# A two-layer graph network on one core: destination rows loaded a quad at a time, index loads spread over three quads, and the last layer's bias on TensorE

## The chip, the core and the metric

The kernel runs on one core of one Trainium2 chip. The core has TensorE (matmuls, PE in the profile), VectorE (DVE), ScalarE (ACT), GpSimd (POOL) and SyncE (SP), which here only issues transfers. The metric is device time in microseconds (us), less is better.

## The reference

There are 6250 nodes with 128 features, 200000 edges sorted by destination, and 128 features for each edge. Two layers follow each other, each with a residual and a layer norm of its own.

```python
src, dst = edge_index
# layer 0
m_in = concat([h_node[src], h_node[dst], h_edge])
m    = silu(m_in @ msg_W1 + msg_b1) @ msg_W2 + msg_b2
agg  = segment_sum(m, dst)
h0   = layernorm(x + (silu(concat([x, agg]) @ upd_W1 + upd_b1) @ upd_W2 + upd_b2)) * gamma + beta
x1   = layernorm(x + h0)
# layer 1
agg  = segment_sum(x1[src], dst) / max(degree, 1)
h    = relu(relu(concat([x1, agg]) @ W1 + b1) @ W2 + b2)
out  = layernorm(x1 + h)
```

## The kernel before

**Stages.** First (up to about 76 us) the products P = x·W(source part) and Q = x·W(destination part) of all nodes are made and stored in HBM as `P_d` and `Q_d`. Then one pass goes over the edges. An edge tile is 128 edges, a quad is 4 tiles (`QT`), a group is 7 quads (`GQ`), there are 391 quads (`NQ`) in 56 groups (`GROUPS`). The loop variable `s` is the quad, `g, q = divmod(s, GQ)`. Nodes are in blocks of 128.

**One quad.** TensorE makes `ps_pre` (`products`, L1135 for the edge features, L1138 for the destination part by `Qw`, a window of rows of Q, times the 0/1 matrix `nodeE`). VectorE adds the gathered rows of P (L948, `pre<-ps_pre,gath`), ScalarE takes the silu (L1328), and TensorE sums the hidden rows by destination (`sums`, L1172, L1174). TensorE also counts, for layer 1, how many edges run from each node to each window of destinations (`count`, L1152), ScalarE copies the counts (L1288), and SyncE stores them as `A_d` (L766). VectorE makes the 0/1 matrices `edgeL` and `edgeK` (L933, L935) and `nodeE` (L925) from keys that `make_keys(g + 1)` (L900 to L909) builds once a group at q == 2 from `src_i`, `dst_i` and `first_i`.

**Loads.** GpSimd gathers rows of P for group g + 1, four for each quad (L876, an indirect DMA each): for quad q once the vector add of quad q of group g is done (it frees `gath[:, q]`), the first also once `src_i` is there. All other loads of the pass are issued by SyncE in the order of its program and lie in one queue: `rel_c` and `eT_c` for chunks of two quads (L759, L761, the latter waits for `pre_mm`, TensorE's products), at q == 1 `load_ids(g + 1)`: `src_i`, `dst_i`, `first_i` (L749 to L751) and then `load_q(g + 1)`, which reads a start row from the table `gbase` into a register (L740) and loads `Qw` in two transfers, quad 0 (30 KB, L743) and quads 1 to 6 (180 KB, L744). Stores of `A_d` and loads of `A_v` (L781, blocks of the stored counts for layer 1) stand in between.

**Layer 1.** Units of four node blocks of layer 0 are finished along the way (`unit_step`). "Visits" (L1188, planned in `VISITS`) multiply count blocks with finished features x1 and VectorE adds them to `sumT` (L965). The output of layer 1 is made in 13 units `w` of four blocks (`LAST_UNITS`), each in steps k of `L_STEPS`, which `plan_last` lays over the last quads and the visits behind them: k 0 TensorE hidden layer (L1246, L1248), k 1 ScalarE relu (L1392), k 2 TensorE second matmul into `ps_y` (L1255), k 3 VectorE bias (L1051), max and residual (L1055), statistics (L1059, L1064), k 4 ScalarE root (L1398), k 5 VectorE (L1069, L1070), k 6 ScalarE normalisation (L1404), store (L1407) and the loads of a later unit (L1379, L1380). In the profile some buffers of the last layer have the names of buffers whose place they take: `ps_cnt` is `ps_y`, `gath` is `xT_l` or `x_l`, `eT_c` is `z_l`, `pre` is `hT_l`, `counts` and `edgeK` are late visit blocks. `l_z` counts VectorE's two steps of k 3, which let TensorE write `ps_y` again.

```python
first = 0
for w in range(len(LAST_UNITS)):
    first = max(first, start[VISITS[LAST_VISIT[w]][0] + 1] + 2)
    steps += [(next(s for s in start if start[s] >= first + t), first + t, w, k) for k, t in enumerate(L_STEPS)]
    first += 4
```

## Time and profile before

| | |
|---|---|
| runs | 3142.61, 3161.31, 3148.67 us; median 3148.67 us |
| the profiled execution's own time | 3123.57 us |
| its span | 3121.4 us |
| TensorE busy | 2325.1 us, 74% |
| weight loads busy | 1965.8 us, 63% |
| VectorE busy | 1681.4 us, 54% |
| ScalarE busy | 1430.8 us, 46% |
| GpSimd busy | 1505.4 us, 48% |
| mean granted TensorE clock | 0.79 |
| HBM | 155 GB/s over the span |

The span runs from the first to the last instruction of the profiled execution. Busy shares are means over the whole span; a mean of 74% hides stretches at 100% and others far below. What an engine waited for is told by its group's releaser; "remote" is a releaser that the profile doesn't know, "issue" is time in which the engine waited for nothing that the profile shows.

### The profile page before, as it was taken

The numbers are of one execution on the slowest core, as the hardware profiler recorded it, in microseconds if no ns is written. First come the engines' busy times: TensorE is split into PE (matmuls) and PEld (weight loads), VectorE is DVE, ScalarE is ACT, GpSimd is POOL, SyncE is SP. The second block draws the span as 40 slices with busy tenths as digits, with TensorE's granted clock in tenths as the row PEclk, the third lists the DMA queues.
The fourth block names the chain that finished last, engine by engine and source line by source line (L and its number), as shares of the span: only waits on it lengthen the run. The fifth ranks groups of instructions, "written<-read, shape, count | busy, mean of one in ns | idle before, by whom it ended". The sixth has DMA issues, their size and how long they took to land.

```text
span 3121.4 us, 59783 instructions
## 1 busy us (share of the span) xinstructions
PE 2325.1 (74%) x19638; PEld 1965.8 (63%) x19638; DVE 1681.4 (54%) x5628; ACT 1430.8 (46%) x3734; POOL 1505.4 (48%) x1605
## 2 busy tenths in 40 slices
PE   6767786877877777777866877776857777877974
PEld 6655665665666666666755666665756666666863
DVE  5555555655555555555645555554645555554543
ACT  2544554544544544545544544543534444454412
POOL 4555555555455545445545554445454544545010
PEclk8877767877876877878877877887878788888996
DMA  6444444544454544455544555554555555556662
GB/s 221 122 136 143 135 138 142 162 138 150 139 166 142 154 141 151 141 160 160 167 145 151 163 161 167 168 161 149 165 161 154 157 172 156 175 183 178 190 224 65
DMA packets 307524, 487.82 MB, mean 156 GB/s; under 512 B 120203, under 2 KB 181645, under 8 KB 307209
## 3 DMA queue, kind: packets, MB, share of 16 engines
q1 hardware_dynamic: 240926, 368.52, 38.2%
q0 software_dynamic: 50016, 102.53, 11.9%
q10 hardware_dynamic: 16266, 12.88, 1.3%
q8 instruction: 160, 2.62, 0.3%
q14 instruction: 156, 1.27, 0.1%
HBM read 375.62 MB, written 108.13 MB: 155 GB/s over the span
## 4 chain that ended last, share of the span: by engine, by line
PE 49%; issue 18%; another core or an unknown queue 14%; DVE 9%; ACT 7%; DMA 1%; DVEq 1%; ACTq 0%; SPq 0%; POOL 0%; POOLq 0%
PE ps_pre L1135 12%; PE ps_cnt L1152 11%; PE ps_l L1188 8%; PE ps_sum L1172 8%; DVE edgeK L935 3%; PE ps_pre L1138 3%; ACT counts L1288 2%; DVE edgeL L933 2%; PE ps_sum L1174 1%; ACT farN L1308 1%; ACT h L1328 1%; DVE pre L948 1%; DMA gath<-x1T_d 1%; DVE sumT L965 1%
## 5 line engine op out<-in xcount | busy, mean ns | idle before, releaser
L876 POOL DMA_INDIRECT gath<-P_d,src_i x1535 | 1454.6, 948 | 1400.1 <-DVE pre L948 541.4
L1135 PE MATMUL ps_pre<-wc,eT_c 128*128 128x128 f32 x3128 | 720.1, 349 | 91.0 <-issue 89.5
L948 DVE TENSOR_TENSOR pre<-ps_pre,gath 128x512 f32<-128x512 f32 x384 | 263.4, 686 | 954.2 <-remote 725.2
L1152 PE MATMUL ps_cnt<-edgeK,edgeL 128*128 128x250 bf16 (+1 forms) x3128 | 568.3, 333 | 206.8 <-issue 105.8
L1135 PEld LDWEIGHTS ps_pre<-wc,eT_c 128*128 128x128 f32 x3128 | 582.8, 229 | 138.3 <-issue 106.0
L935 DVE TENSOR_SCALAR edgeK<-iotaK,key 128x500 bf16<-128x500 f16 (+1 forms) x1564 | 667.4, 488 | 0.0
L1288 ACT ACTIVATE counts<-ps_cnt 128x1000 bf16<-128x1000 f32 x391 | 405.4, 1037 | 417.1 <-remote 296.9
L1172 PE MATMUL ps_sum<-edgeN,h 128*128 128x40 f32 x3128 | 476.0, 300 | 104.8 <-issue 100.1
L1172 PEld LDWEIGHTS ps_sum<-edgeN,h 128*128 128x128 f32 x3128 | 449.3, 216 | 125.2 <-issue 109.5
L1152 PEld LDWEIGHTS ps_cnt<-edgeK,edgeL 128*128 128x128 bf16 x3128 | 315.0, 110 | 317.5 <-issue 221.2
L1188 PE MATMUL ps_l<-A_v,x1h 128*128 128x120 bf16 x4856 | 356.8, 230 | 143.4 <-issue 132.0
L1318 ACT ACTIVATE edgeN<-farN 128x160 f32<-128x160 f32 x391 | 128.5, 329 | 675.4 <-remote 552.5
L1188 PEld LDWEIGHTS ps_l<-A_v,x1h 128*128 128x128 f16 x4856 | 309.7, 106 | 178.4 <-issue 169.8
L1138 PE MATMUL ps_pre<-Qw,nodeE 120*128 120x128 bf16 x1564 | 381.5, 244 | 53.3 <-issue 52.9
L1308 ACT ACTIVATE farN<-iotaN,rel_g 128x40 f32<-128x40 f16 x1564 | 378.5, 313 | 2.6 <-issue 2.3
L1328 ACT ACTIVATE h<-pre 128x512 f32<-128x512 f32 x391 | 244.3, 625 | 271.2 <-DVE pre L948 207.5
L933 DVE TENSOR_SCALAR edgeL<-iotaL,low 128x132 bf16<-128x132 f16 x1564 | 328.1, 271 | 0.0
L965 DVE TENSOR_TENSOR sumT<-ps_l,sumT 128x120 f32 x432 | 120.4, 279 | 319.3 <-remote 191.7
L1138 PEld LDWEIGHTS ps_pre<-Qw,nodeE 120*128 120x128 bf16 x1564 | 177.5, 113 | 63.9 <-issue 63.8
L1174 PE MATMUL ps_sum<-edgeB,onesb 128*128 128x40 bf16 x1564 | 116.8, 187 | 50.6 <-issue 50.5
L1174 PEld LDWEIGHTS ps_sum<-edgeB,onesb 128*128 128x128 bf16 x1564 | 118.2, 127 | 57.5 <-issue 57.5
L925 DVE TENSOR_SCALAR nodeE<-rel_c,pidq 120x512 bf16<-120x512 bf16 x391 | 136.4, 349 | 0.1
(159 smaller groups left out, 1467.6 us busy)
## 6 DMA issues: line engine op xcount, KB each, us to landing
eT_c<-eT SPq DMA_DIRECT2D x196, 512.0 KB
A_d<-counts SPq DMA_DIRECT2D x168, 384.0 KB
rel_c<-rel_d SPq DMA_DIRECT2D x196, 240.0 KB
A_v<-A_d SPq DMA_DIRECT2D x70, 448.0 KB
A_v<-A_d SPq DMA_DIRECT2D x111, 256.0 KB
gath<-P_d,src_i POOLq DMA_INDIRECT x1535
A_d<-counts SPq DMA_DIRECT2D x56, 416.0 KB
Qw<-Q_d SPq DMA_DIRECT2D x56, 180.0 KB
```

Of the source, the lines that this page charges most:

```text
L876: pool.indirect_dma_start(gath[:, q, t * D:(t + 1) * D], None, v["P_d"], bass.IndirectOffsetOnAxis(ap=src_i[g % 2][:, c:c + 1], axis=0)).t ...
L933: V.tensor_scalar(edgeL[x][:, j, :], iotaL[:, :, 0:LC], low[k][:, q * QT + j:q * QT + j + 1], None, ALU.is_equal)
L935: last = V.tensor_scalar(edgeK[x][:, ROFF[j]:ROFF[j] + A2 * w], iotaK[j][:, :, 0:A2 * w // KR], key[k][:, q * QT + j:q * QT + j + 1], None ...
L948: V.tensor_tensor(pre[s % 2][:], ps_pre[s % 2][:], gath[:, q, :], ALU.add).then_inc(pre_add, 1)
L1135: T.matmul(o, eT_c[c % RE][:, e0:e0 + P], wc[:], start=True, stop=False)
L1138: last = T.matmul(o, nodeE[x][:, t * P:(t + 1) * P], Qw[g % 2][:, q, :], start=False, stop=True)
L1152: last = T.matmul(o[:, :, w0:w0 + w], edgeL[x][:, j, 0:P], r, start=(j == 0), stop=(j == QT - 1 and q == 0), skip_group_check=True)
L1172: T.matmul(ps_sum[:, cols], h[x][:, t, :], edgeN[x][:, t, :], start=False, stop=True, skip_group_check=True)
L1188: last = T.matmul(l1_part(i), x1h[:, a, part, :], A[:, (a - lo) * P:(a - lo) * P + GW], start=(a == lo and part == 0), stop=(a == hi - 1 a ...
L1288: A.activation(counts[k][:].rearrange("p (b a) d -> p b a d", b=2)[:, :, :, bass.ds(off, W0)], ps_cnt[:, :, 0:AB * W0].rearrange("p b (a d ...
L1308: last = A.activation(farN[:, j, :], iotaN[:, q, :, 0:WN // KR], ACT.Square, scale=-1.0, bias=rel_g[k][:, q * QT + j:q * QT + j + 1])
L1328: A.activation(h[x][:, :, 0:D], pre[x][:].rearrange("p (t n) -> p t n", n=D), ACT.Silu).then_inc(silu, 1)
```

## The change

Three things. `load_q` loads one quad of `Qw` (30 KB) instead of a group; SyncE does it in every quad for the quad seven later, behind the edge loads, and each quad has a semaphore of its own, on which TensorE waits in every quad. The index loads of a group come at q = 1 (`src_i`), 2 (`dst_i`) and 3 (`first_i`), and the keys are built at q = 4. In the last layer TensorE puts the bias b2 into `ps_y` by a matmul of `ones_row` with `b2bc` ahead of the second matmuls, which then add to it, and VectorE's L1051 goes; `L_STEPS` and the distance of units in `plan_last` are closer.

```diff
--- before.py
+++ after.py
@@ -109,7 +109,7 @@
 VISITS_AT = {s: [i for i, v in enumerate(VISITS) if v[0] == s] for s, d, lo, hi in VISITS}
 UNIT_AT = {s0 + k: (u, k) for u, (lo, hi, s0) in enumerate(UNITS) for k in range(-4, U_LEN + 1)}
 LAST_VISIT = [max(i for i, (s, d, b0, b1) in enumerate(VISITS) if 112 * d - SLACK < P * hi) for lo, hi in LAST_UNITS]
-L_STEPS = (0, 2, 3, 5, 9, 10, 11)
+L_STEPS = (0, 2, 3, 5, 8, 9, 10)
 
 
 def plan_last():
@@ -123,7 +123,7 @@
     for w in range(len(LAST_UNITS)):
         first = max(first, start[VISITS[LAST_VISIT[w]][0] + 1] + 2)
         steps += [(next(s for s in start if start[s] >= first + t), first + t, w, k) for k, t in enumerate(L_STEPS)]
-        first += 4
+        first += 3.2
     return sorted(steps, key=lambda step: step[1])
 
 
@@ -697,7 +697,7 @@
     zrow, onesb = v["zrow"], v["onesb"]
     e_in, i_in, r_in = v["e_in"], v["i_in"], v["r_in"]
     s_in = [sem(f"s_in{k}") for k in range(2)]
-    q_in = [sem(f"q_in{k}") for k in range(2)]
+    q_in = [sem(f"q_in{q}") for q in range(GQ)]
     c_out = [sem(f"c_out{k}") for k in range(2)]
     prepared = sem("prepared")
     turn_mm, turned = v["turn_mm"], v["turned"]
@@ -736,20 +736,27 @@
     def sync(sp):
         v["settled"](sp)
 
-        def load_q(g):
+        def load_q(g, q):
+
+            if g >= 1:
+                sp.wait_ge(q_in[q], 16 * g)
+            if g >= 2:
+                sp.wait_ge(pre_mm, (g - 2) * GQ + q + 1)
             base = sp.value_load(gbase[0:1, g:g + 1], min_val=0, max_val=NP_ - 1)
-            first = v["Q_d"][bass.ds(base, WN), :]
-            rest = v["Q_d"][bass.ds(base + NLO[1], WN), :]
-            sp.dma_start(Qw[g % 2][:, 0, :], bass.AP(first.tensor, first.offset, [[D, KQ], [1, D]])).then_inc(q_in[g % 2], 16)
-            sp.dma_start(Qw[g % 2][:, 1:GQ, :], bass.AP(rest.tensor, rest.offset, [[D, KQ], [3 * D * (NLO[2] - NLO[1]), GQ - 1],
-                                                                                [1, D]])).then_inc(q_in[g % 2], 16)
-
-        def load_ids(g):
-            k = g % 2
-            sp.dma_start(src_i[k][:], v["src_pt"][:, g * GT:(g + 1) * GT]).then_inc(s_in[k], 16)
-            sp.dma_start(dst_i[k][:], v["dst_pt"][:, g * GT:(g + 1) * GT]).then_inc(i_in[k], 16)
-            sp.dma_start(first_i[k][:], v["dst_first"][g * GT:(g + 1) * GT].partition_broadcast(P)).then_inc(i_in[k], 16)
-            load_q(g)
+            rows = v["Q_d"][bass.ds(base + NLO[q], WN), :]
+            sp.dma_start(Qw[g % 2][:, q, :], bass.AP(rows.tensor, rows.offset, [[D, KQ], [1, D]])).then_inc(q_in[q], 16)
+
+        def load_sources(g):
+
+            sp.dma_start(src_i[g % 2][:], v["src_pt"][:, g * GT:(g + 1) * GT]).then_inc(s_in[g % 2], 16)
+
+        def load_destinations(g):
+
+            sp.dma_start(dst_i[g % 2][:], v["dst_pt"][:, g * GT:(g + 1) * GT]).then_inc(i_in[g % 2], 16)
+
+        def load_firsts(g):
+
+            sp.dma_start(first_i[g % 2][:], v["dst_first"][g * GT:(g + 1) * GT].partition_broadcast(P)).then_inc(i_in[g % 2], 16)
 
         def load_chunk_of(s):
 
@@ -825,15 +832,20 @@
                 sp.dma_start(deg[:, cols], v["rdeg_d"][cols].partition_broadcast(P)).then_inc(dg_io, 16)
 
         def fast():
-            load_q(0)
-            load_ids(1)
+            for q in range(GQ):
+                load_q(0, q)
+            load_sources(1)
+            load_destinations(1)
+            load_firsts(1)
             v["table_stored"](sp)
             for s in range(ENDQ):
                 g, q = divmod(s, GQ)
                 load_chunk_of(s)
-                if q == 1 and 1 <= g < GROUPS - 1:
+                if g < GROUPS - 1 and s + GQ < NQ:
+                    load_q(g + 1, q)
+                if 1 <= q <= 3 and 1 <= g < GROUPS - 1:
                     sp.wait_ge(sum_mm, g * GQ)
-                    load_ids(g + 1)
+                    (load_sources, load_destinations, load_firsts)[q - 1](g + 1)
                 if 1 <= q <= len(PARTS) and 1 <= g <= GROUPS:
                     store(g - 1, q - 1)
                 unit_loads(s)
@@ -1048,13 +1060,10 @@
                 dve.wait_ge(l_y, w + 1)
                 if w >= 3:
                     dve.wait_ge(l_out[w % 3], 16 * (w // 3))
-                V.tensor_tensor(z, ps_y[x][:, 0:n * D].rearrange("p (j n) -> p j n", n=D),
-                                b2bc[:].unsqueeze(1).broadcast_to([P, n, D]), ALU.add).then_inc(l_z, 1)
-                dve.wait_ge(l_z, 2 * w + 1)
                 dve.wait_ge(l_x_in[w % 3], 16 * (w // 3 + 1))
-                V.scalar_tensor_tensor(z, z, 0.0, x_l[w % 3].rearrange("p (j n) -> p j n", n=D)[:, 0:n, :], ALU.max,
+                V.scalar_tensor_tensor(z, ps_y[x][:, 0:n * D].rearrange("p (j n) -> p j n", n=D), 0.0, x_l[w % 3].rearrange("p (j n) -> p j n", n=D)[:, 0:n, :], ALU.max,
                                        ALU.add).then_inc(l_z, 1)
-                dve.wait_ge(l_z, 2 * w + 2)
+                dve.wait_ge(l_z, w + 1)
                 for j in range(n):
                     last = V.bn_stats(st_l[:, j, :], z[:, j, :])
                 l_link(last)
@@ -1092,7 +1101,7 @@
                 for i in VISITS_AT.get(s - 1, ()):
                     add_visit(i)
                 unit_step(s)
-                if g + 1 < GROUPS and q == 2:
+                if g + 1 < GROUPS and q == 4:
                     make_keys(g + 1)
                 if g + 1 < GROUPS and q == 5:
                     clear(g + 1)
@@ -1122,8 +1131,7 @@
             c, x = s // CQ, s % 2
             if s % CQ == 0:
                 pe.wait_ge(e_in[c % RE], 16 * (c // RE + 1))
-            if q == 0:
-                pe.wait_ge(q_in[g % 2], 32 * (g // 2 + 1))
+            pe.wait_ge(q_in[q], 16 * (g + 1))
             pe.wait_ge(nodes, s + 1)
             if s < GQ:
                 pe.wait_ge(turned, s + 1)
@@ -1250,9 +1258,11 @@
                 n, x = last_columns(w)[1], w % 2
                 pe.wait_ge(l_relu, w + 1)
                 if w >= 2:
-                    pe.wait_ge(l_z, 2 * (w - 2) + 1)
+                    pe.wait_ge(l_z, w - 1)
+                T.matmul(ps_y[x][:, 0:n * D], ones_row[:], b2bc[0:1, :].unsqueeze(1).broadcast_to([1, n, D]), start=True, stop=True)
                 for j in range(n):
-                    last = T.matmul(ps_y[x][:, j * D:(j + 1) * D], hT_l[x][:, j * P:(j + 1) * P], w2[:], start=True, stop=True)
+                    last = T.matmul(ps_y[x][:, j * D:(j + 1) * D], hT_l[x][:, j * P:(j + 1) * P], w2[:], start=False, stop=True,
+                                    skip_group_check=True)
                 last.then_inc(l_y, 1)
 
         def fast():
@@ -1375,7 +1385,7 @@
                 act.wait_ge(x1T_out, 16 * len(UNITS))
             if w >= 3:
                 act.wait_ge(l_hidden, w - 2)
-                act.wait_ge(l_z, 2 * (w - 2))
+                act.wait_ge(l_z, w - 2)
             act.dma_start(xT_l[r][:, 0:n * P], v["x1T_d"][:, cols]).then_inc(l_xT_in[r], 16)
             act.dma_start(x_l[r].rearrange("p (j n) -> p j n", n=D)[:, 0:n, :],
                           v["x1_d"][cols, :].rearrange("(j p) n -> p j n", p=P)).then_inc(l_x_in[r], 16)
```

SyncE's program where the loads of group 10 begin, in quad 1 of group 9 (`nodes`, `pre_mm`, `sum_mm`, `cnt_copy` are counts of VectorE, TensorE, TensorE and ScalarE). Before:

```order
L759 DMA rel_c<-rel_d 120x1024 [waits nodes]
L761 DMA eT_c<-eT 128x1024 [waits pre_mm]
L749 DMA src_i<-src_pt 128x28 [waits sum_mm]
L750 DMA dst_i<-dst_pt 128x28
L751 DMA first_i<-dst_first 128x28
L740 TENSOR_LOAD gbase
L740 ISA x2
L743 ISA
L743 DMA Qw<-Q_d 120x128
L744 ISA
L744 DMA Qw<-Q_d 120x6x128
L766 DMA A_d<-counts 128x1664 [waits cnt_copy]
```

The same place now:

```order
L747 DMA Qw<-Q_d 120x128
L766 DMA rel_c<-rel_d 120x1024 [waits nodes]
L768 DMA eT_c<-eT 128x1024 [waits pre_mm]
L745 TENSOR_LOAD gbase [waits pre_mm,q_in1]
L745 ISA x2
L747 ISA
L747 DMA Qw<-Q_d 120x128
L751 DMA src_i<-src_pt 128x28 [waits sum_mm]
L773 DMA A_d<-counts 128x1664 [waits cnt_copy]
L745 TENSOR_LOAD gbase [waits pre_mm,q_in2]
```

A register load and one Qw transfer have moved ahead of `src_i`; `dst_i` and `first_i` have moved behind the store of `A_d`.

TensorE's program near the last visits, where the counts of slot 6 are multiplied (`av_in6` is their load). Before:

```order
L1188 MATMUL ps_l<-counts,x1h 128x120 [waits sums_changed,un_lo,av_in6]
L1188 MATMUL ps_l<-counts,x1h 128x120 x3
L1255 MATMUL ps_cnt<-l_w,pre 128x128 [waits l_z,l_relu]
L1255 MATMUL ps_cnt<-l_w,pre 128x128 x3
L1246 MATMUL ps_pre<-gath,l_w 128x512 [waits l_xT_in0,l_relu]
L1248 MATMUL ps_pre<-sumT,l_w 128x512 [waits l_mean]
L1188 MATMUL ps_l<-counts,x1h 128x120 [waits sums_changed,un_lo,av_in7]
L1188 MATMUL ps_l<-counts,x1h 128x120 x9
```

The same place now:

```order
L1196 MATMUL ps_l<-counts,x1h 128x120 [waits sums_changed,un_lo,av_in6]
L1196 MATMUL ps_l<-counts,x1h 128x120 x3
L1262 MATMUL ps_cnt<-l_b,ones_row 128x512 [waits l_z,l_relu]
L1264 MATMUL ps_cnt<-l_w,pre 128x128 x4
L1254 MATMUL ps_pre<-gath,l_w 128x512 [waits l_xT_in1,l_relu]
L1256 MATMUL ps_pre<-sumT,l_w 128x512 [waits l_mean]
L1196 MATMUL ps_l<-counts,x1h 128x120 [waits sums_changed,un_lo,av_in7]
L1196 MATMUL ps_l<-counts,x1h 128x120 x9
```

The bias matmul (L1262) stands ahead of the four second matmuls and takes over their wait, and the hidden layer between the same visits is that of unit 7 (feature buffer 1, `l_xT_in1`) where it was that of unit 6 (`l_xT_in0`).

## Rows read from the trace of the kernel before

**Rows 1.** The page: TensorE's busy time, and the chain by engine.

```profile
PE 2325.1 (74%) x19638; PEld 1965.8 (63%) x19638; DVE 1681.4 (54%) x5628; ACT 1430.8 (46%) x3734; POOL 1505.4 (48%) x1605
...
PE 49%; issue 18%; another core or an unknown queue 14%; DVE 9%; ACT 7%; DMA 1%; DVEq 1%; ACTq 0%; SPq 0%; POOL 0%; POOLq 0%
```

**Rows 2.** Windows: length, busy us (instructions), granted clock, DMA share, GB/s.

```profile
core 0: us, PE busy (x) PEld busy (x) DVE busy (x) ACT busy (x) POOL busy (x), PEclk, DMA share, GB/s
...
1520.50:1524.50 4.00, 3.58 (x47) 3.11 (x46) 3.79 (x13) 3.85 (x10) 3.07 (x4) 1.00 0.73 199
1524.50:1537.50 13.00, 5.57 (x19) 3.03 (x19) 2.37 (x13) 1.58 (x6) 8.28 (x9) 0.55 0.41 82
```

**Rows 3.** Waits of GpSimd: total us, times, longest.

```profile
POOL gath L876 <- DMA src_i<-src_pt: 399.5, 45, 19.0
```

**Rows 4.** Windows of groups 23 and 32, from one group's first add to the next's.

```profile
1200.70:1245.00 44.30, 33.28 (x241) 28.16 (x239) 23.89 (x77) 22.36 (x61) 24.71 (x27) 0.73 0.51 153
1664.10:1718.10 54.00, 33.50 (x241) 27.98 (x239) 26.45 (x86) 22.76 (x64) 27.70 (x30) 0.71 0.47 146
```

**Rows 5.** Timeline of GpSimd: first gathers of five groups, with the wait before.

```profile
1210.01 0.95 POOL L876 DMA_INDIRECT gath<-P_d,src_i  x1 [5.45 <-DMA src_i<-src_pt]
...
1418.31 0.95 POOL L876 DMA_INDIRECT gath<-P_d,src_i  x1 [3.23 <-DMA src_i<-src_pt]
...
1520.52 0.95 POOL L876 DMA_INDIRECT gath<-P_d,src_i  x1 [9.50 <-DMA src_i<-src_pt]
...
1679.57 0.95 POOL L876 DMA_INDIRECT gath<-P_d,src_i  x1 [11.26 <-DMA src_i<-src_pt]
...
2105.48 0.95 POOL L876 DMA_INDIRECT gath<-P_d,src_i  x1 [19.04 <-DMA src_i<-src_pt]
```

**Rows 6.** SyncE's two largest waits: total us, times, longest.

```profile
SPq L761 <- PE ps_pre L1138: 540.7, 56, 25.2
...
SPq L781 <- PE ps_l L1188: 513.6, 104, 20.7
```

**Rows 7.** Timeline of SyncE: groups 27, 29 and 40, the index and Qw loads.

```profile
1416.34 0.33 SPq L749 DMA_DIRECT2D src_i<-src_pt  x1
...
1517.60 0.47 SPq L749 DMA_DIRECT2D src_i<-src_pt  x1
...
1518.59 0.43 SPq L751 DMA_DIRECT2D first_i<-dst_first  x1
1519.96 0.40 SPq L743 DMA_DIRECT2D Qw<-Q_d  x1
1520.55 0.37 SPq L744 DMA_DIRECT2D Qw<-Q_d  x1
...
2098.99 0.43 SPq L749 DMA_DIRECT2D src_i<-src_pt  x1
```

**Rows 8.** Line 1131, TensorE's waits in `products`: ns min/median/max, first and last start.

```profile
L1131 PEldq EVENT_SEMAPHORE  x389: 51/51/51, 90.8 to 2925.8; - x195
```

**Rows 9.** Timeline of VectorE in group 23: the keys, and two adds.

```profile
1224.72 0.18 DVE L900 TENSOR_TENSOR rel_g<-dst_i,first_i 128x28 f32<-128x28 int32 x1
...
1225.67 0.69 DVE L948 TENSOR_TENSOR pre<-ps_pre,gath 128x512 f32<-128x512 f32 x1
...
1233.92 0.69 DVE L948 TENSOR_TENSOR pre<-ps_pre,gath 128x512 f32<-128x512 f32 x1 [4.92 <-remote]
```

**Rows 10.** Lines 1051 and 1209, the bias add and layer 0's bias matmul: ns min/median/max.

```profile
L1051 DVE TENSOR_TENSOR eT_c<-ps_cnt,l_b x13: 291/681/693, 2992.5 to 3108.4; 128x512 f32<-128x512 f32 x12, 128x128 f32<-128x128 f32 x1
...
L1209 PE MATMUL ps_u<-ub2bc,ones_row x26: 371/685/1056, 338.9 to 2940.9; 1*128 1x512 f32 x22, 1*128 1x256 f32 x2, 1*128 1x384 f32 x2
```

**Rows 11.** The chain behind the last visit, one cycle: start us, us, what.

```profile
3064.28 3.08 DMA gath<-x1T_d
...
3067.49 2.05 PE ps_pre L1246 x2
3069.54 1.72 PE ps_pre L1248 x2
...
3071.97 1.54 ACT eT_c L1404 x4
```

**Rows 12.** Timeline of TensorE: the hidden layers of units 8 and 11.

```profile
3067.49 2.05 PE L1246 MATMUL ps_pre<-gath,l_w 128*128 128x512 f32 x2 [7.06 <-DMA gath<-x1T_d]
...
3096.81 2.04 PE L1246 MATMUL ps_pre<-gath,l_w 128*128 128x512 f32 x2 [2.91 <-DMA gath<-x1T_d]
```

## The prediction

> **What bounds the kernel now.** I read the page first: TensorE is busy 74% of the span and 49% of the chain that ended last, but 18% of the chain is "issue" and 14% a releaser that the profile doesn't name [rows 1]. No engine is full, so the next question is when TensorE is slow. The windows show it: in 1520.50 to 1524.50 it gets through 47 matmuls in 4 us, busy 3.58, clock granted 1.00; in the next 13 us, while GpSimd's gathers follow each other, it gets through 19, is busy 5.57 us, and the clock falls to 0.55 [rows 2]. That is 1.5 matmuls per us instead of 12. The gathers of a group (28, a group ahead) start when two things are there: the vector add of quad 0 of the group before, which frees the buffer, and the group's source indices. They then catch up with a backlog of one to three quads, and this long stretch of gathers is where the group loses time. GpSimd waited for the index load 45 times, 399.5 us in all, 19.0 at the longest [rows 3], 8.9 us a time.
>
> So what a later index load costs can be read from groups with equal work. Groups 23 and 32 both have 241 matmuls: 44.30 and 54.00 us [rows 4]. Their first gathers start after waits of 5.45 and 11.26 us for the load [rows 5]. That is 9.70 us for 5.81 us later. The same sum over all 54 groups (by each group's length against the time from its first vector add to its first gather) is less steep, 0.87 us per us, with about 0.16 of uncertainty. I use 0.9.
>
> SyncE itself has room. Its two largest waits are for TensorE at the edge loads, 540.7 us in 56, and at the visit loads, 513.6 us in 104 [rows 6]; together 1054 us, 19 us a group.
>
> **The destination rows by quad.** In group 29 SyncE is done with the third index load at 1519.02 (1518.59 and 0.43) and issues the two Qw loads until 1520.92 [rows 7]: 1.90 us a group. The first, register load and address included, ends at 1520.36, so one costs 1.34 us. Seven cost 9.38, 7.5 us more a group, against 19 us of waits: hidden, as long as nothing urgent stands behind it. Something does: the source indices. In the changed order one Qw load now stands between the edge loads and src_i; before, all of them stood behind it. Some 54 groups by 1.34 us are 72 us of later issue. How much of it arrives? The load of src_i lies in the same queue as 512 KB of eT_c and 240 KB of rel_c, issued just ahead. With them ahead, gather follows issue by 2.92 us (1517.60 to 1520.52) or 6.49 (2098.99 to 2105.48, with visit loads ahead as well); where no edge load stood right ahead, it follows by 1.97 (1416.34 to 1418.31) [rows 5, 7]. So with an edge load ahead the data wait in the queue, and issuing 1.34 us later uses up the 1 to 4.5 us that they would have waited (2.92 and 6.49 less 1.97). I take 0.1 us for 47 groups in which the queue is the limit, 4.7, and a full 1 us for 7 in which, as I estimate, SyncE doesn't wait between two quads, so that two Qw loads fall ahead: 11.7 us in all. By 0.9 this is **+10 us**. The bounds: 0 if the queue takes it all, and 72 by 0.9, +65, if nothing is taken.
>
> The Trainium skill, "DMA: Bandwidth & Descriptors", Rules for kernel authors, speaks against the split: many small transfers are to be coalesced, under 64 KB they are mostly overhead, and its section on the anatomy of one DMA gives a fixed cost of some 2 us. The change makes 279 more transfers of 30 KB; by that figure 558 us if each were waited for. The same rules say to issue early and wait late, and no row of the kernel before shows TensorE waiting for Qw in the loop; a Qw quad is issued seven quads ahead here.
>
> TensorE gets one more wait on some 196 quads. Such an instruction takes 51 ns [rows 8], 10 us if all were exposed. It lies on the queue that feeds the weight loads and would be hidden wherever that queue runs ahead. I take 0 and keep 10 for the range.
>
> **The index loads over three quads, and the keys two quads later.** Destination indices and firsts come one and two quads later than before (a quad is a seventh of 44.30 us, 6.3). Who reads them is the key building on VectorE: from 1224.72 to 1225.67, 0.95 us, after which the vector add of quad 3 starts with no wait; the add of quad 4 of the same group, at 1233.92, had waited 4.92 us [rows 9]. Moved to quad 4, the keys are built before an add that in this group comes after the long stretch too. Where the add at quad 3 was late because of them, 0.95 us come off the path; where it was waiting anyway, nothing. Between 0 and 54 by 0.95, −51 us, I take 0: the adds that follow the burst wait for a releaser that isn't VectorE, and the gathers behind the add are already queued for time. If first_i landed late, VectorE would stand still with the add of quad 5 behind it, and the gathers and ScalarE behind that. A little over one quad, some 6 to 7 us, is left for it, and even with visit loads ahead src_i took 6.49: so 0, and only groups that TensorE runs through fast could pay a us or two.
>
> **The last layer.** The 13 vector adds of the bias go, 8.5 us of VectorE; 13 times TensorE gets a bias matmul of one row by 512 columns, of which the like now takes 0.68 us for one pass of two [rows 10], so about 1.4 us each. While visits still run, TensorE pays 8 of them, 6 to 11 us by the shortest (0.371) and the mean pass, and VectorE is spared 8 by 0.68. Behind the last visit the units run by a cycle: the load of the next unit's features 3.08 us, the hidden layer 2.05 and 1.72, and ScalarE's normalisation 1.54, with its activation and the issue between [rows 11]. From 3067.49 to 3096.81 three units pass, 9.8 us each, and TensorE is idle 2.9 to 7 us ahead of each [rows 12]. The vector add is not in this cycle, and the bias matmul falls into TensorE's idle time. The steps of neighbouring units keep their order on each engine, so the cycle stays 9.8 us. What changes is how many units are left: the pieces of TensorE's order show unit 7's hidden layer ahead of the visit where unit 6's stood. One cycle fewer behind the visits is −9.8. The denser units cost among the visits: bias matmuls and waits for loads that are now nearer, +4 by my estimate (half of the bias matmuls, since the other half falls into idle time there too). Together **−6 us**, between −12 (nothing paid) and +4 (bias paid in full, and the unit gained lost to its own load).
>
> At the start SyncE has seven Qw loads ahead of the loop, but TensorE needs only the first: 0.
>
> **Sum.** The profiled execution took 3123.57 us: +10 −6 gives 3127.6. It lies 25 us under the median of the runs shown (3148.67; 3142.61 to 3161.31), and runs are compared with that, so the forecast is 3148.67 + 4, about **3152 us**. Half a per cent, 16 us, is about what a measurement can tell from no change: 3133 to 3164.
>
> **The rivals.**
> *A, slower: the later index load arrives in full.* The Qw load ahead of src_i costs 1.34 us in each group and the queue gives none of it back. For it: GpSimd waits for this load in 45 of 54 groups, so there is no other slack. Against it: the 1.97 us where the queue is free. It gives +65 −6, 3208; it decides (past 3164) as soon as a third of the 72 us arrives, and with half of it the time is about 3175.
> *B, faster: VectorE's key building was on the path at quad 2 or the lighter queue helps.* For it: the add with no wait at 1225.67. If half of the 51 us comes off, 3148.67 − 26 + 10 − 6 = 3127. Against it: the add a quad later waits anyway.
> *C, slower: SyncE or the small transfers become the bound.* 7.5 us a group more against 19 of waits; only if waits of some groups are all spent. A fifth of the groups paying in full: 11 by 7.5, 83 us, about 3235.
> *D, the stretches of gathers don't set the group's time.* Then a later start costs nothing and the tail is left: 3148.67 − 6, about 3143.
>
> **How the numbers follow.** My forecast 0.39 and D 0.06, which both lie within half a per cent; A 0.24; B 0.25; C 0.06. A with less than a third arriving stays within the bound and counts as my forecast. The range 3120 to 3188 takes in B at half and a little more, A with up to 70% of the 72 us arriving, and TensorE's 10 us for the waits on top of my own case; it leaves out A in full, C, and B in full. The likeliest case alone: 3137 to 3166. Faster 0.25, same 0.45, slower 0.30.
>
> **What would show it.** In the changed profile: GpSimd's wait for src_i at 400 to 450 us (A: over 450); first gathers 3 us behind the issue of src_i in groups with an edge load ahead falling towards 2; 391 Qw loads and SyncE's two large waits some 400 us smaller; TensorE never waiting for Qw; the adds of quad 3 starting after a wait of their own; 26 bias matmul passes; four units and not five behind the last visit, each still 9.8 us. I am wrong if the issue of src_i to the first gather stays what it was (A), if the lengths of groups don't follow their first gather (D), or if the add at quad 3 comes 1 us sooner throughout (B).

## The result: 2.2% slower, outside the range

The changed kernel took 3217.86 us (median of 4 runs, 3215.82 to 3221.43) against 3148.74 us before (4 runs): a ratio of 1.0216, 95% interval 1.0183 to 1.0248. The forecast was 3152 with a range to 3188; the nearest number on record is rival A's 3208. A second series of the same kernel gave a ratio of 1.016 (1.0121 to 1.02); its medians, 3215.07 against 3155.77, take in one run of 3251.57 us that the ratio leaves out. The experiments ran in one of two conditions, the kernel before in them too: it took 3097 to 3156 us in one and about 2210 us in the other. Every ratio below is taken within its own series.

The page of the changed kernel, its span, TensorE's busy time, the chain by engine, and the gathers:

```profile
span 3219.7 us, 62198 instructions
...
PE 2327.6 (72%) x19664; PEld 1961.9 (61%) x19664; DVE 1670.3 (52%) x5615; ACT 1424.3 (44%) x3734; POOL 1498.7 (47%) x1605
...
PE 49%; issue 17%; another core or an unknown queue 17%; ACT 7%; DVE 7%; DMA 2%; ACTq 1%; DVEq 1%; SPq 0%; POOL 0%; POOLq 0%
...
L888 POOL DMA_INDIRECT gath<-P_d,src_i x1535 | 1450.2, 945 | 1497.0 <-DVE pre L960 574.6
```

TensorE does the same work in a longer time [rows 1]. The waits of GpSimd for the source indices, and SyncE's two large ones:

```profile
POOL gath L888 <- DMA src_i<-src_pt: 510.0, 50, 50.4
```

```profile
SPq L768 <- PE ps_pre L1146: 499.9, 69, 22.2
SPq L788 <- PE ps_l L1196: 404.7, 118, 20.1
```

The longest, 50.4 us, is the gather that opens the edge pass, which before was put down to VectorE; without it 460 us in 49 waits stand against 399.5 in 45 [rows 3]. SyncE's waits have shrunk [rows 6] and are still large: it isn't the bound.

Where the 98 us between the two profiled executions lie (3219.7 and 3121.4 us of span) is best seen by stage. Cut at the first product of group 1, the first product of group 55 and the last visit, the windows of the kernel before (columns as in [rows 2]) are

```profile
0.00:125.30 125.30, 87.46 (x514) 81.24 (x515) 70.64 (x171) 47.81 (x97) 57.80 (x81) 0.82 0.54 177
125.30:2903.00 2777.70, 2081.61 (x17432) 1758.40 (x17430) 1518.03 (x5112) 1326.15 (x3503) 1431.92 (x1511) 0.79 0.52 155
2903.00:3059.30 156.30, 129.60 (x1637) 111.94 (x1635) 74.78 (x276) 40.22 (x94) 13.95 (x11) 0.93 0.61 195
3059.30:3121.40 62.10, 26.44 (x66) 14.19 (x63) 17.95 (x72) 16.66 (x41) 1.68 (x2) 0.55 0.24 68
```

and those of the changed one

```profile
0.00:132.80 132.80, 88.21 (x513) 82.17 (x514) 70.42 (x170) 47.65 (x97) 55.62 (x81) 0.82 0.52 167
132.80:2993.70 2860.90, 2072.23 (x17433) 1754.38 (x17430) 1517.66 (x5114) 1319.66 (x3503) 1427.53 (x1511) 0.78 0.51 151
2993.70:3167.40 173.70, 142.68 (x1665) 113.89 (x1663) 69.19 (x269) 42.87 (x100) 13.90 (x11) 0.91 0.56 179
3167.40:3219.70 52.30, 24.51 (x64) 11.50 (x60) 13.07 (x66) 14.13 (x35) 1.68 (x2) 0.61 0.23 66
```

The start is 7.5 us longer, the 54 groups 83.2 us, the stretch to the last visit 17.4 us, and what is behind it 9.8 us shorter. The profiled execution of the kernel before lies 25 us under the median of its runs, so some of the 83 us may be chance in that execution; the medians differ by 69.

Why the groups are longer shows in SyncE's timeline of group 9, where the loads of group 10 begin:

```profile
532.83 0.36 SPq L768 DMA_DIRECT2D eT_c<-eT  x1
534.17 1.72 SPq L747 DMA_DIRECT2D Qw<-Q_d  x2
535.94 0.37 SPq L751 DMA_DIRECT2D src_i<-src_pt  x1
```

and in GpSimd's:

```profile
538.33 0.94 POOL L888 DMA_INDIRECT gath<-P_d,src_i  x1 [7.54 <-DMA src_i<-src_pt]
```

The same loads and the same gather before:

```profile
514.09 0.33 SPq L761 DMA_DIRECT2D eT_c<-eT  x1
514.47 0.43 SPq L749 DMA_DIRECT2D src_i<-src_pt  x1
...
517.97 0.95 POOL L876 DMA_INDIRECT gath<-P_d,src_i  x1 [5.77 <-DMA src_i<-src_pt]
```

The load of `src_i` was issued 0.38 us behind that of `eT_c`, and the first gather began 3.88 us behind it. Now two Qw loads stand in between: 3.11 us from load to load, and 5.50 us to the gather. So the issue came 2.73 us later in this group, and the gather 1.62. Two Qw loads stand ahead in every odd group, since an edge load serves two quads and falls in quad 0 there, ahead of both; in even groups it falls in quad 1 and one Qw load is between. (The two pieces of SyncE's order shown ahead of the prediction are those of an even group, not of group 9.)

The means over all groups, counted from the traces. The first three columns run from the end of the vector add that frees the buffer, or from the issue, in us, odd and even groups apart. A long run is nine or more gathers with less than 0.5 us between them, within the 54 groups; the last column is how many matmuls TensorE starts per us in them.

| kernel | add to issue of src_i | issue to first gather | add to first gather | all groups | long runs | matmuls per us |
|---|---|---|---|---|---|---|
| before | 1.68, 4.86 | 3.45, 4.24 | 5.13, 9.10 | 7.11 | 43, 715 us | 3.9 |
| changed | 3.75, 5.76 | 2.70, 3.77 | 6.45, 9.54 | 7.99 | 51, 851 us | 3.7 |
| changed, second series | 3.74, 6.22 | 2.54, 3.97 | 6.27, 10.19 | 8.23 | 49, 822 us | 3.7 |
| src_first_8 (below) | 1.81, 4.62 | 3.73, 4.41 | 5.54, 9.03 | 7.29 | 46, 768 us | 3.8 |
| src_early_3 (below) | a group ahead | a group ahead | 1.06, 0.93 | 0.99 | 1, 14 us | 4.9 |

The first gather of a group begins 1.3 us later in the 27 odd groups and 0.4 in the 27 even ones, in the second series 1.1 and 1.1. Long runs take 136 and 107 us more. In the shorter runs and outside runs TensorE starts about 7.1 matmuls per us, so by my estimate from these rates the longer runs cost 65 and 51 us, of the 83 and 77 us by which the groups are longer in the two traces. The time shows at one place in the odd groups: from the vector add of quad 2 to that of quad 3 it was 10.1 us and is 13.3 (13.0 in the second series; 11.0 in `src_first_8`).

### The profile page after: what moved, and what is told of

It is laid out like the page before. It is cut to its first block, busy times and chain, and to the rows that moved or that the text cites. A ratio compares the mean times of both kernels' runs of the same rounds, so it can differ in the third digit from the quotient of the medians.

```text
span 3219.7 us, 62198 instructions
## 1 busy us (share of the span) xinstructions
PE 2327.6 (72%) x19664; PEld 1961.9 (61%) x19664; DVE 1670.3 (52%) x5615; ACT 1424.3 (44%) x3734; POOL 1498.7 (47%) x1605
## 4 chain that ended last, share of the span: by engine, by line
PE 49%; issue 17%; another core or an unknown queue 17%; ACT 7%; DVE 7%; DMA 2%; ACTq 1%; DVEq 1%; SPq 0%; POOL 0%; POOLq 0%
PE ps_pre L1143 12%; PE ps_cnt L1160 11%; PE ps_l L1196 9%; PE ps_sum L1180 7%; PE ps_pre L1146 3%; DVE edgeK L947 3%; ACT counts L1298 3%; DVE edgeL L945 1%; ACT farN L1318 1%; ACT h L1338 1%; DMA gath<-x1T_d 1%; PE ps_sum L1182 1%; DVE pre L960 1%; PE ps_u L1220 1%
## 5 line engine op out<-in xcount | busy, mean ns | idle before, releaser
L1143 PE MATMUL ps_pre<-wc,eT_c 128*128 128x128 f32 x3128 | 702.2, 346 | 65.8 <-issue 65.5
L1143 PEld LDWEIGHTS ps_pre<-wc,eT_c 128*128 128x128 f32 x3128 | 574.4, 227 | 104.2 <-issue 72.4
```

Source lines behind the costliest of these rows:

```text
L1143: T.matmul(o, eT_c[c % RE][:, e0:e0 + P], wc[:], start=True, stop=False)
```

## The experiments

All ratios are to the kernel before in the same series.

| label | kernel | this, us | before, us | ratio (95%) |
|---|---|---|---|---|
| tail_only | last layer's part alone | 2217.64 | 2209.41 | 1.0042 (1.0029 to 1.0055) |
| loads_only | load part alone | 2210.67 | 2209.41 | 1.0008 (0.9999 to 1.0017) |
| after_src_first | changed, src_i ahead of Qw | 2221.86 | 2209.41 | 1.0052 (1.0039 to 1.0065) |
| src_early | before, src_i a group ahead | 2205.0 | 2209.41 | 0.9977 (0.9966 to 0.9988) |
| after_again | changed | 3215.07 | 3155.77 | 1.016 (1.0121 to 1.02) |
| loads_only_2 | as loads_only | 2210.86 | 2210.6 | 0.9998 (0.9986 to 1.0009) |
| src_first_2 | as after_src_first | 2219.03 | 2210.6 | 1.0034 (1.0023 to 1.0045) |
| src_early_2 | as src_early | 2208.08 | 2210.6 | 0.9979 (0.9964 to 0.9995) |
| src_first_3 | as after_src_first | 2217.94 | 2208.55 | 1.0035 (1.0023 to 1.0048) |
| steps_only | closer steps alone | 2220.95 | 2208.55 | 1.0049 (1.003 to 1.0067) |
| src_early_3 | as src_early | 2931.6 | 3108.75 | 0.9408 (0.9362 to 0.9454) |
| src_first_4 | as after_src_first | 2221.05 | 2213.48 | 1.0033 (1.0021 to 1.0046) |
| src_first_5 | as after_src_first | 2220.58 | 2213.52 | 1.003 (1.0017 to 1.0042) |
| after_src_early | changed, src_i a group ahead | 2214.72 | 2212.0 | 1.0015 (1.0006 to 1.0024) |
| src_first_6 | as after_src_first | 2221.49 | 2212.0 | 1.0047 (1.0033 to 1.0061) |
| src_first_7 | as after_src_first | 2220.23 | 2210.42 | 1.0041 (1.0023 to 1.0059) |
| src_first_8 | as after_src_first | 3133.98 | 3110.51 | 1.0085 (1.0052 to 1.0118) |
| early_bias | src_early with the bias on TensorE | 2918.67 | 3096.66 | 0.9429 (0.9377 to 0.9481) |

**The two parts apart.** Theory: the loss is in the loads. Rival: it is in the last layer. `tail_only` has the bias matmul and the closer steps, `loads_only` all the rest.

> The kernel before with the last layer's part of the change alone (bias by TensorE, steps and units closer). By my prediction's term the tail gives -6 us (-12 to +4), so about 3143. The profile after the whole change suggests otherwise: start 7 us later, 54 groups 83 us more, so 7 to 8 us are left for the tail: 3156. Rival: most of the loss is here, above 3180.

> The changed kernel with the last layer as before, so the load part alone (Qw by quad, index loads over three quads, keys at quad 4). Theory: the loss is here, 3205 to 3212, with GpSimd waiting some 510 us for src_i. Rival (tail is the loss): 3155.

> The load part of the change alone (Qw by quad, index loads over three quads, keys at quad 4; the last layer as before), run again for a chip on which TensorE has the slow stretches. There: if the load part is the loss, 3205 to 3212 against 3150, and the tail the 8 us that it cost on the other chip. On a chip without the slow stretches: 2210 again.

Both series of `loads_only` fell into the 2210 us condition. The loads cost nothing that can be told from zero there (1.3 and 0.3 us). The profile of `loads_only` looks quite different from that of the condition of record: its chain, and the waits of the gathers.

```profile
POOL 45%; PE 21%; issue 17%; DMA 7%; DVE 7%; DVEq 1%; ACT 1%; SPq 0%; ACTq 0%; POOLq 0%
```

```profile
POOL gath L888 <- issue: 457.0, 1499, 0.3
...
POOL gath L888 <- DMA src_i<-src_pt: 24.1, 2, 18.5
```

GpSimd sets the time there: 28 gathers at 1.25 us are 35 us, and a group takes 34.9 (1884.70 us for 54, below). It is always behind, so the indices have long been there when it comes to them. The tail's 8 us stay. The stages of `tail_only` from group 1 on,

```profile
101.00:1984.10 1883.10, 1751.86 (x17431) 1554.68 (x17430) 1504.42 (x5102) 1308.84 (x3499) 1422.57 (x1500) 0.93 0.76 228
1984.10:2163.10 179.00, 145.91 (x1664) 117.20 (x1663) 73.20 (x273) 42.77 (x100) 25.17 (x23) 0.90 0.58 181
2163.10:2215.80 52.70, 24.57 (x65) 11.58 (x62) 13.15 (x66) 14.13 (x35) 1.67 (x2) 0.61 0.23 65
```

and of `loads_only`,

```profile
101.00:1985.70 1884.70, 1748.34 (x17431) 1546.65 (x17430) 1508.74 (x5102) 1303.35 (x3499) 1422.46 (x1500) 0.94 0.76 228
1985.70:2147.70 162.00, 131.69 (x1637) 114.09 (x1636) 78.24 (x279) 40.25 (x94) 25.12 (x23) 0.93 0.62 196
2147.70:2209.40 61.70, 24.26 (x65) 12.62 (x63) 17.93 (x72) 16.65 (x41) 1.67 (x2) 0.58 0.24 68
```

put these 8 us where the changed kernel has its own: 17.0 us more before the last visit, 9.0 less behind it. Both expectations of 3150 and more can't be judged by the times of this series; the tail's size can.

**The changed kernel once more.**

> The changed kernel itself, run once more. In the runs so far the kernel before took 2209 us where the run of record took 3149, with no stretch in which TensorE is slow while gathers follow each other. If this run is again under such conditions: the sum of the two parts measured there (loads +1, tail +8), 2219. If it is under the conditions of record: 3218 against 3149.

The loss of record holds: 1.6%, which is 50 us, and 59 by the medians.

**src_i ahead of the Qw loads.** The changed kernel, only the order in SyncE's loop is different:

```diff
-                if g < GROUPS - 1 and s + GQ < NQ:
-                    load_q(g + 1, q)
                 if 1 <= q <= 3 and 1 <= g < GROUPS - 1:
                     sp.wait_ge(sum_mm, g * GQ)
                     (load_sources, load_destinations, load_firsts)[q - 1](g + 1)
+                for late in ((), (0, 1), (2,), (3,), (4,), (5,), (6,))[q]:
+                    if g < GROUPS - 1 and (g + 1) * GQ + late < NQ:
+                        load_q(g + 1, late)
```

> The changed kernel with the Qw loads of quads 0 and 1 issued behind the load of src_i; all else as changed. Theory: what costs is the later issue of src_i (by the changed profile 1.5 us a group later, 0.9 us later first gather): 54 groups by 0.9 by 0.9 us, 44 us back, about 3175, and GpSimd's wait for src_i back to 400 us. Rival (the keys at quad 4, or the waits of TensorE in every quad): no more than 10 us back, above 3205.

> The changed kernel with src_i ahead of the Qw loads of quads 0 and 1, for a chip with the slow stretches. If the later src_i is the cause, its issue comes back by 1.5 us a group, the first gather by 0.9 to 1.1 us, and 45 to 50 us come off: 3170. If the keys at quad 4 or the waits of TensorE are the cause, above 3205.

> The changed kernel with src_i ahead of the Qw loads of quads 0 and 1, for a chip with the slow stretches (kernel before 3110 to 3156 there, the changed one 1.6 to 2.2% above it). If the later issue of src_i is the cause, 45 us come back: a ratio of 1.003 to 1.008. If it is the keys at quad 4, the waits or the transfers: above 1.014.

Seven of the eight runs (after_src_first, src_first_2 to src_first_7) gave 1.003 to 1.0052 at 2218 to 2222 us, the tail's price and nothing else: where the gathers set the time, the order of these loads makes no difference that these runs show. The eighth, src_first_8, ran in the condition of record.

> As src_first_4: with slow stretches 1.003 to 1.008 if the later issue of src_i is the cause, above 1.014 if not; without them 1.0035.

Its ratio is 1.0085 (1.0052 to 1.0118), at the edge of what the theory of the late `src_i` gave and clear of the rival's 1.014. GpSimd's wait for the source indices is nearly back to what it was:

```profile
POOL gath L889 <- DMA src_i<-src_pt: 445.9, 50, 41.2
```

Without the one that opens the pass it is 404.7 us, where the kernel before had 399.5 and the changed one 459.6. The issue of `src_i`, the first gathers and the long runs are nearly back too (the table above). Its stages:

```profile
0.00:126.30 126.30, 88.40 (x515) 82.40 (x515) 70.58 (x170) 47.77 (x97) 58.02 (x81) 0.81 0.55 176
126.30:2902.40 2776.10, 2071.88 (x17430) 1746.79 (x17429) 1518.17 (x5113) 1321.27 (x3503) 1429.42 (x1511) 0.79 0.54 155
2902.40:3079.70 177.30, 144.64 (x1666) 115.33 (x1663) 69.47 (x269) 42.93 (x100) 13.91 (x11) 0.91 0.56 176
3079.70:3132.60 52.90, 24.48 (x64) 11.53 (x61) 13.08 (x66) 14.13 (x35) 1.68 (x2) 0.61 0.23 65
```

The groups are back at 2776.1 us, where the kernel before had 2777.7 and the changed one 2860.9. What is left is the tail, 21.0 us more and 9.2 less, 11.8 in all or 0.38%. Of the 0.85% some 0.5% (0.1 to 0.8 by the interval, 4 to 25 us) isn't the tail: this series' kernel before (3110.51) was itself quicker than that of record, and no trace of it in this series tells where. So the later `src_i` carries 0.75 to 1.3% (1.016 and 1.0216 less 1.0085), 23 to 41 us, about half of the loss and its largest part. The difference is one between series, and the intervals of 1.016 and 1.0085 (1.0121 to 1.02 and 1.0052 to 1.0118) only just keep apart; that gathers, waits and groups return together in the trace is the stronger evidence. The keys, the waits and the transfers together may carry up to those 25 us; they are all still in this kernel, and which of them costs stays open.

**src_i a group ahead.** The kernel before with a third buffer, so that the gathers never wait for it:

```diff
-            src_i = [sb(f"src_i{k}", [P, GT], I32, both) for k in range(2)]
+            src_i = [sb(f"src_i{k}", [P, GT], I32, both) for k in range(3)]
...
-                pool.wait_ge(s_in[g % 2], 16 * ((g + 1) // 2))
+                pool.wait_ge(s_in[g % 3], 16 * ((g + 2) // 3))
...
                     load_ids(g + 1)
+                    if g + 2 < GROUPS:
+                        load_sources(g + 2)
```

> The kernel before with a third src_i buffer, loaded a whole group earlier, so that the gathers never wait for it; nothing else changed. If a later first gather costs 0.9 us per us also down to zero, 7.1 us a group come off: 54 by 0.9 by 7.1, -345 us, 2805. If only the part behind the backlog counts, some -100, 3050. Rival (the stretches of gathers don't set the time of a group): 3140 to 3155.

> The kernel before with src_i loaded a group ahead, for a chip with the slow stretches. A straight line through the groups gives 0.9 us per us for 7.1 us: 2805. If only the backlog's length counts (one quad instead of two, 46.8 instead of 51.4 us a group) it gives 54 by 4.6, 248 us: 2900. If the stretches don't set a group's time: 3150.

> The kernel before with src_i loaded a group ahead, for a chip with the slow stretches: 2900 if the backlog's length is what counts, 2805 on a straight line, 3150 if a late start of the gathers doesn't matter. Without slow stretches 2206 again.

At 2210 us it is 0.2% faster. In the condition of record it takes 2931.6 us instead of 3108.75, −5.9%. GpSimd's waits no longer name the indices,

```profile
POOL gath L882 <- DVE pre L954: 750.0, 264, 8.3
POOL gath L882 <- issue: 407.7, 1265, 1.9
```

and the 54 groups take

```profile
124.40:2711.70 2587.30, 2075.45 (x17430) 1762.49 (x17429) 1517.69 (x5112) 1325.51 (x3502) 1431.22 (x1511) 0.81 0.57 167
```

with the same gathers and the same matmuls: 190 us less than in the trace of the kernel before, which is from another series (within this one the medians differ by 177). The long runs of gathers are gone, all but one. The start of the gathers does set the length of a group. The straight line (2805, 345 us less) promised nearly twice of what came: 190 us for 6.1 us a group of earlier start (7.11 to 0.99, 54 groups, 330 us) is 0.58 us per us.

**The changed kernel with src_i a group ahead.**

> The changed kernel with src_i loaded a group ahead into a third buffer. With slow stretches: src_early alone gave 0.941 of the kernel before. If the later src_i is all that costs in the loads, the tail's 8 us are left: 0.944. If keys, waits or transfers cost on their own: the remaining 1.2 to 1.8%, 0.953 to 0.959. On a chip without slow stretches: 2206 and the tail's 8 to 10: 2215.

It ran in the 2210 us condition and took 2214.72 us, as expected there: 0.36% above `src_early_2` (1.0015 less 0.9979), about the tail's price. For the condition of record it says nothing.

**The tail taken apart.** `steps_only` changes the two numbers alone (`L_STEPS` and 3.2).

> The kernel before with the last layer's steps and units set closer alone, the bias left on VectorE. If the closer units are what cost the tail its 8 us (TensorE waits for loads that come later among the visits, and the visits end later): +7 to +9 us. If the bias matmuls do it (26 passes of 0.37 to 0.68 us, 10 to 18 us, half hidden): 0 to +2 us here.

It costs 12.4 us by the medians, where 7 to 9 were expected of it, and at least as much as steps and bias together (8.2 in another series, the intervals overlap): the closer steps are the tail's loss, and the bias on TensorE costs nothing that these intervals can tell. The waits of `steps_only` between 2065.0 us and the last visit,

```profile
PEld ps_pre L1246 <- issue: 28.3, 6, 7.1
PE ps_pre L1246 <- DMA gath<-x1T_d: 27.4, 6, 6.9
```

and of `loads_only`, steps as before, between the same time and its last visit,

```profile
PEld ps_pre L1257 <- issue: 7.4, 4, 3.5
PE ps_pre L1257 <- DMA gath<-x1T_d: 6.7, 3, 3.3
```

differ by 20.7 us of TensorE standing before the hidden layer of a unit whose features haven't landed, with the visits queued behind it.

**The version that the runs point to.** `src_early` and the bias on TensorE, steps and Qw loads as before.

> The kernel before with src_i a group ahead and the last layer's bias on TensorE; steps and Qw loads as before. With slow stretches: 0.941 as src_early, within 0.002. Without: 0.998 as src_early if the bias costs nothing; if the bias matmuls were half exposed, 4 to 9 us more, 1.000 to 1.002. The stage from group 55 to the last visit should be 156 to 162 us, not the 174 to 182 of the closer steps.

It ran in the condition of record: 2918.67 against 3096.66 us, ratio 0.9429 (0.9377 to 0.9481), the same as `src_early_3` (0.9408) within the intervals. Its stages from group 55 on:

```profile
2685.90:2840.80 154.90, 133.08 (x1651) 110.24 (x1649) 70.17 (x271) 40.27 (x94) 13.93 (x11) 0.97 0.63 196
2840.80:2903.50 62.70, 32.58 (x78) 14.99 (x75) 14.20 (x66) 16.77 (x41) 1.68 (x2) 0.60 0.24 67
```

TensorE is busy 6 us longer in the first than in `src_early_3` (126.94 of 156.00 us) and the stretch, at 154.9 us, is no longer (156 to 162 was expected). Either version beats the kernel before by some 6%, and the changed one, by the ratios (0.943 against 1.016 and 1.0216), by 7 to 8%.

## Why the prediction was wrong, point by point

**What bounds the kernel: right in kind.** The start of the gathers sets the length of a group: `src_early_3` shows it with 190 us, `src_first_8` by giving the groups back. That it does so by the long runs of gathers, in which TensorE is slow, fits the five traces of the table in the main: the two with the latest start have the most long runs and the longest groups, and the one with the earliest start has a single long run and the shortest groups. No experiment changes the long runs alone, so this part is argued and not shown. Rival D is out.

**The Qw loads ahead of src_i: the failed step.** "I take 0.1 us for 47 groups in which the queue is the limit, 4.7, and a full 1 us for 7 in which, as I estimate, SyncE doesn't wait between two quads, so that two Qw loads fall ahead: 11.7 us in all." Two things in it failed. The count: two Qw loads fall ahead in 27 groups and not 7, for a reason that is in the code and not in SyncE's waits, the Qw load of quad 0 behind the edge load in every odd group. And the overlap with the queue, which weighed more: it was to give back nine tenths in 47 groups, and it gave back between a third and four tenths. The issue came 2.1 us later in odd groups and 0.9 in even ones (2.1 and 1.4 in the second series), 80 and 92 us in all, near the 72 of the prediction; the wait from issue to first gather fell by only 0.75 and 0.47 us (0.91 and 0.27). What arrived is 48 and 60 us of later start, where the sum had 11.7. With the count put right and the prediction's own shares (27 by 1 and 27 by 0.1) it would have been 30. The upper bound of 72 was slightly low because of the count.

**The price of a us: not shown to be wrong.** 0.9 came from a comparison of groups. The groups lost 83 and 77 us for 48 and 60 us of later start, 1.7 and 1.3 us per us, but that puts everything down to it and compares traces of several series. The order alone carries 23 to 41 us by the ratios, for 51 and 38 us of later start (8.23 and 7.99 less 7.29, 54 groups): 0.5 and 1.1. The earlier start gives 0.58. With the measured start the prediction's own sum gives 43 to 54 us for the loads and, with the tail's 7.6 below, 51 to 62 us in all, where 50 to 69 were measured. So the step that failed is the arrival, and not the price.

**Rival A: near in number, not in kind.** Its 3208 needs all of 72 us to arrive and a tail of −6. What arrived is 48 to 60, and the tail brought a loss: that 3218 lies so near is in part chance. One of its signs came, a wait of GpSimd over 450 us (460); the other, the same time from issue to gather as before, didn't: that time fell, as the forecast had it, only by less.

**SyncE's room, and 279 more transfers: right.** The Qw transfers are 391 now; TensorE's waits list none for Qw. SyncE's two large waits, with those of the same lines that the profile puts down to no known releaser, went from 2010.5 to 1521.5 us, where "some 400 us smaller" was forecast. What the rule on small transfers (the Trainium skill, "DMA: Bandwidth & Descriptors", Rules for kernel authors) would cost, waited for one by one, didn't come: issued seven quads ahead they are hidden, as the same section's advice to issue early has it. (The 2 us behind the prediction's 558 are given in the same page of the Trainium skill, in the section on the anatomy of one DMA, for transfers that GpSimd issues; these are SyncE's.) Their price was SyncE's issue time in front of one urgent load.

**The keys at quad 4, TensorE's extra waits: 0 taken.** `loads_only` shows no cost at 2210 us (1.3 and 0.3 us). In the condition of record up to 25 us for both and the transfers remain possible. VectorE waited for `first_i` twice, 4.2 us in all, as allowed for. Rival B's sign appears in part and brings nothing: in even groups the vector add of quad 3 comes sooner behind that of quad 0 (17.6 us, 20.9 before) and the one of quad 4 no sooner (33.4 and 32.9); in odd groups quad 3 comes later (23.7 and 21.9).

**The tail: one half right, the other mis-sized.** Behind the last visit one cycle fewer was to bring −9.8 us, and it brought −9.8 (62.1 to 52.3; four units, 9.5 and 9.7 us from one full unit to the next). That it fits to the tenth is luck: it was −9.2 in `src_first_8` and −9.0 between `loads_only` and `tail_only`. Among the visits "+4 by my estimate" was 17.4. The term took the bias matmuls for the cost and put their half at 4; by `steps_only` it is the waits for the loads. Together the tail is +7.6 in this trace, where −6 was forecast. TensorE's rows of the changed kernel among the last visits,

```profile
3136.74 1.10 PE L1254 MATMUL ps_pre<-gath,l_w 128*128 128x512 f32 x2 [1.56 <-DMA gath<-x1T_d]
...
3147.75 2.05 PE L1254 MATMUL ps_pre<-gath,l_w 128*128 128x512 f32 x2 [3.98 <-DMA gath<-x1T_d]
...
3160.79 2.04 PE L1254 MATMUL ps_pre<-gath,l_w 128*128 128x512 f32 x2 [4.21 <-DMA gath<-x1T_d]
```

show the wait, and behind a wait of 4 us a hidden layer of 2.05 us instead of 1.10, as in [rows 12]. The granted clock is 0.50 from 3147.80 to 3149.50 and 1.00 from 3136.80 to 3138.60: the lower of the chip's two levels, 1.2 GHz, in place of 2.4. The load that is waited for starts only when ScalarE has normalised an earlier unit, so units closer together make the cycle of [rows 11] rule among the visits too (11.0 and 13.0 us from one of these hidden layers to the next), and the visits wait in TensorE's order.

**The start: 7.5 us, taken as 0.** Some 6 of them are there before the first product of the pass (86.3 us, 80.2 before; 86.7 in the second series), while the preparation runs, in code that the change leaves alone; in `src_first_8` they are absent (79.7) with the same seven loads. So at most 1.5 us are the loads'; the rest is open.

## What to carry to other kernels

An urgent small load pays for everything that is issued ahead of it on its queue's engine: when transfers are split and strewn through a loop, list for each kind of iteration what now stands between the event that starts the urgent load and its issue. Loading such a thing an iteration earlier, here for one buffer of 112 bytes a partition, was worth more in the condition of record (5.9%) than ordering it well (0.75 to 1.3%). A schedule with less distance between dependent units gains behind the last filler work and can lose more in front of it (9.8 against 17.4 us here), if the in-order engine that waits also carries the filler.

## What the hardware showed that was not expected

The same program runs in two conditions. In 25.00 to 40.00 us, where the preparation's gathers follow each other, `tail_only` (2210 us condition) shows

```profile
25.00:40.00 15.00, 14.60 (x64) 14.41 (x63) 13.57 (x14) 7.03 (x9) 13.17 (x7) 1.00 0.92 340
```

and `early_bias` (condition of record)

```profile
25.00:40.00 15.00, 5.98 (x25) 5.50 (x24) 5.48 (x5) 2.63 (x3) 11.95 (x11) 0.55 0.35 116
```

25 matmuls instead of 64, the clock granted 0.55 instead of 1.00, transfers at 116 GB/s instead of 340; and the kernel before takes 40% more time as a whole. A gather by itself takes the same (949 ns in `loads_only`, 945 in the changed kernel's row). Both traces come from one and the same chip, in series some time apart (2209 and 3097 us for the kernel before), so it isn't a trait of single chips, as the expectations above took it to be. What switches it, and why TensorE's instructions come slowly while gathers run, no run here shows. It decides what a change is worth: the load part of this one costs 0% in one and some 1.2 to 1.8% in the other (1.016 and 1.0216 less the tail's 0.38%, since `loads_only` never ran there), and the earlier `src_i` brings 0.2% and 5.9%.
